# Two graph layers on one core: in layer 0, the next tile's target scores are computed between the maximum and the shift of the softmax

## What is computed

```python
h = einsum('bnd,ade->bane', feat_in, W)
th = tanh(h)
attn = einsum('bane,aeo->bano', th, w_src) + swapaxes(einsum('bane,aeo->bano', th, w_dst), 2, 3)
attn = where(attn >= 0, attn, 0.2 * attn)
attn = softmax(where(~adj, -999.0, attn), axis=-1)
feat_out = elu(einsum('banm,bame->bane', attn, h) + b)
gate = sigmoid(feat_in @ H_w.T + H_b)
return gate * feat_out + (1 - gate) * feat_in
```

## Time and profile before

| what | value |
|---|---|
| runs | 2766.51, 2765.05, 2766.31 us; median 2766.31 |
| the profiled execution's own time | 2766.33 us |
| its span (first to last instruction) | 2764.6 us |
| TensorE matmul busy | 2726.9 us, 99% of the span |
| VectorE busy | 1668.8 us, 60% |
| ScalarE busy | 1160.3 us, 42% |
| GpSimd busy | 1066.3 us, 39% |
| granted TensorE clock | 0.997 of full speed |

### The profile page before, as it was taken

How to read it: one execution, slowest core, us unless ns; L and a number is a source line. 1 busy time by engine, 2 the same in 40 slices (tenths; PEclk the granted TensorE clock), 3 DMA queues, 4 the chain that set the end, 5 groups by cost and what they waited for, 6 DMA issues and landing times.

```text
span 2764.6 us, 51821 instructions
## 1 busy us (share of the span) xinstructions
PE 2726.9 (99%) x20988; PEld 2517.8 (91%) x20988; DVE 1668.8 (60%) x3334; ACT 1160.3 (42%) x3045; POOL 1066.3 (39%) x630
## 2 busy tenths in 40 slices
PE   8999999999999989999999999999999999999998
PEld 6877778888788889999999999999999999999998
DVE  6888998888888754444454444454445445444443
ACT  5666776666666633322332233322332233223322
POOL 2453344433444134433444343434443343434340
PEclk9999999999999999999999999999999999999999
DMA  5656665555555512222213222222222222222220
GB/s 180 173 131 145 164 160 145 139 139 139 141 137 143 175 59 69 69 71 81 70 58 81 76 75 58 79 72 71 69 68 71 81 70 58 81 81 70 58 70 23
DMA packets 306894, 269.49 MB, mean 97 GB/s; under 512 B 227808, under 2 KB 244192, under 8 KB 306656
## 3 DMA queue, kind: packets, MB, share of 16 engines
q1 hardware_dynamic: 306656, 266.19, 35.5%
HBM read 142.65 MB, written 75.89 MB: 79 GB/s over the span
## 4 chain that ended last, share of the span: by engine, by line
PE 85%; DVE 5%; DMA 4%; issue 2%; POOL 2%; ACT 2%; SPq 1%; DVEq 0%; ACTq 0%; POOLq 0%
PE ps_hg L1036 21%; PE ps_a L1199 14%; PE ps_k L70 14%; PE ps_q L70 14%; PE ps_a L70 14%; PE ps_c L1165 2%; PE ps_s L1140 2%; PE ps_pv L1068 1%; DMA dst_all<-dst_scratch 1%; ACT logits L564 1%; PE ps_t L1055 1%; PE ps_pt L1165 1%; DMA dst_scratch<-dst 1%; PE ps_pt L1147 1%; DVE logits L770 1%
## 5 line engine op out<-in xcount | busy, mean ns | idle before, releaser
L1036 PE MATMUL ps_hg<-w_hi,xT 128*128 128x512 f32 x2268 | 745.6, 401 | 8.3 <-DVE h_one L803 8.2
L1036 PEld LDWEIGHTS ps_hg<-w_hi,xT 128*128 128x128 f32 x2268 | 426.1, 188 | 112.6 <-issue 11.3
L1036 PE MATMUL ps_hg<-w_lo,xT 128*128 128x512 f32 x1134 | 448.4, 395 | 0.0
L70 PE MATMUL ps_k<-x1T_hi,wk_hi 128*128 128x256 f32 x1152 | 329.1, 286 | 0.0
L70 PE MATMUL ps_q<-x1T_hi,wq_hi 128*128 128x256 f32 x1152 | 323.5, 281 | 1.4 <-DVE x1T_lo L910 1.4
L70 PE MATMUL ps_q<-x1T_lo,wq_hi 128*128 128x256 f32 x1152 | 322.6, 280 | 0.0
L70 PE MATMUL ps_k<-x1T_lo,wk_hi 128*128 128x256 f32 x1152 | 321.9, 279 | 0.0
L70 PE MATMUL ps_q<-x1T_hi,wq_lo 128*128 128x256 f32 x1152 | 321.9, 279 | 0.0
L70 PE MATMUL ps_k<-x1T_hi,wk_lo 128*128 128x256 f32 x1152 | 321.1, 279 | 0.0
L496 POOL TENSOR_TENSOR th_src<-th,wsrc_all 128x768 f32<-128x768 f32 x64 | 118.3, 1848 | 483.7 <-DVE dst_all L783 463.4
L648 ACT ACTIVATE qT<-ps_q,bq_col 128x256 f32<-128x256 f32 x192 | 80.5, 470 | 479.3 <-PE ps_q L70 479.3
(11 more groups left out here) (144 smaller groups left out, 5814.2 us busy)
## 6 DMA issues: line engine op xcount, KB each, us to landing
x_tok<-x SPq DMA_DIRECT2D x64, 384.0 KB, 4.1
dst_all<-dst_scratch SPq DMA_DIRECT2D x128, 192.0 KB, 3.4
gate_scratch<-gate SPq DMA_DIRECT2D x64, 384.0 KB, 2.6
feat_scratch<-feat SPq DMA_DIRECT2D x128, 192.0 KB, 2.8
feat_in<-feat_scratch SPq DMA_DIRECT2D x62, 384.0 KB, 3.1
gate_in<-gate_scratch SPq DMA_DIRECT2D x62, 384.0 KB, 3.7
x_even<-x SPq DMA_DIRECT2D x16, 768.0 KB, 4.2
x_odd<-x SPq DMA_DIRECT2D x16, 768.0 KB, 4.4
```

Of the source, the lines that this page charges most:

```text
L70: ins = pe.matmul(out, left[a][c], right[b][c], start=(n == 0), stop=(n == len(terms) - 1))
L1036: ins = pe.matmul(ps_hg[:, cols], left[a][c], right[b][c], start=(c == 0 and n == 0), stop=(c == KC - 1 and n == 2))
```

## The change

The shift (line 778) leaves `softmax_scores` and becomes a function of its own, `shift_scores`. In the loop it is called after `dst_scores(T)`, so the target scores of tile T are computed between the maximum and the shift of tile T-1. After the loop, for tile 63, it directly follows `softmax_scores` as before. All waits and signals are the same: the shift waits for `max_done` and raises `shift_done`.

```diff
@@ -774,6 +774,8 @@
                 dve.wait_ge(masked_done, T + 1)
                 dve.tensor_reduce(neg_max[:, :], per_head(logits[:, :], HEADS0), AX_X, ALU.max,
                                   negate=True).then_inc(max_done, 1)
+
+            def shift_scores(T):
                 dve.wait_ge(max_done, T + 1)
                 dve.tensor_tensor(per_head(logits[:, :], HEADS0), per_head(logits[:, :], HEADS0),
                                   over(neg_max[:, :], HEADS0, NODES), ALU.add).then_inc(shift_done, 1)
@@ -881,6 +883,7 @@
                 if T == 1:
                     bias_h(T)
                 dst_scores(T)
+                shift_scores(T - 1)
                 if T >= 2:
                     attention(T - 2)
                     bias_h(T)
@@ -946,6 +949,7 @@
 
             rest_x1(0)
             softmax_scores(NT - 1)
+            shift_scores(NT - 1)
             attention(NT - 2)
             for n in range(3):
                 w1_rest(dve, EARLY_W1 + n)
```

## The result

| | before | after |
|---|---|---|
| median | 2765.68 us (2764.57 to 2766.51) | 2828.06 us (2827.04 to 2830.58) |
| ratio | | 1.0227, 95% interval 1.0209 to 1.0245 |
| span of the profiled execution | 2764.6 us | 2825.5 us |

A forecast was written before the change was run, and what follows sets the result against it. In layer 0 TensorE sets the pace, 14.31 us a tile, until the h_one loop closes at 14.47. +2.8 us to tile 63's multiply and +0.87 at layer 0's end make +3.7 on 2766.33: 2770.0 us, range 2765.0 to 2774.5.

The forecast's parts named there:

- the price of the moved shift: On VectorE behind the target scores' reduction: the shift adds 0.87 us, making multiply to end of h_one 4.81 instead of 3.94.
- the 2.0 us gained at the start: Tiles 1 and 2: multiplies skip the shift ahead of them, so tile 2's comes at 50.48 instead of 52.47.
- the held tiles: Tiles 10 and 12, held by GpSimd's mixing work and late ScalarE: 0.40 and 0.94 us over the loop, written as 1.4.
- The cover that failed: Later work in a tile, GpSimd's product included, was taken as covered by idle time or not delayed, and costed at nothing.
- The loop: Layer 0, each tile: multiply to h_one 4.81, to matmul 0.15, to tanh's end 9.47, to multiply 0.04; 14.47 us against 14.31.
- The 0.87 us at the end of layer 0: Tile 62's shift joins VectorE's chain from tile 63's multiply to the last early weights' split, for which TensorE waits: +0.87 us.
- 0.87 against 0.99: Start-to-start time of VectorE operations: 0.99 us when waiting for the engine's last result, 0.87 otherwise; the forecast took 0.87.
- The exponential: On ScalarE after the shift: ends at 520.12, 0.28 us before the probabilities' weight load at 520.40, so costs nothing.
- The two slower ones (2775.1 and 2777.3): Rivals: VectorE's own length becomes the bound, 2775.1 us, 14%; every VectorE operation costs 0.99 us, 2777.3 us, 2%.
- VectorE's own length: Rival: in tiles with weight splits or mixing work, VectorE's idle time does not absorb the shift; +8.8, 2775.1 us, 14%.
- the forecast's own spread: 2766.8 to 2773.2 us: 1.8 us either way from the loop's terms, 1.4 either way from the held tiles.
- the excess of 0.18 us over what h_one had to spare: In each tile: the shift's 0.87 us exceeds h_one's usable 0.69 us, so the loop closes and 0.16 us is lost.

The follow-up runs named there:

- the two experiments that leave it in its new place: Against the changed kernel: GpSimd's product made to wait for the shift's end, 2782.07 us; or the maximum written to PSUM and read there by the shift, 2773.45 us.
- the PSUM version: The changed kernel with the maximum written to a free PSUM bank, from which the shift reads it: 2773.45 us, ratio 1.0024 to the kernel before.

## Why the prediction was wrong, point by point

- **The step that failed** is the price of the moved shift: "The shift comes behind the reduction, needs the maximum alone, and so costs 0.87 us." That was read from neighbours on VectorE and from what the shift waits for. What ran on another engine at the new place was not asked. The shift costs 1.75 us there, 1.83 less the overlap of some 0.08 with the next instruction, because GpSimd's product, which starts 0.08 us after the multiply's end (515.62 after 515.54), holds it until the product has ended. Put into the forecast's own sum: 61 x (15.35 - 14.47) = 53.7 us for the tiles, 0.88 at the end of layer 0, and 1.5 of the 2.0 us gained at the start were not there (51.99 instead of 50.48). 3.7 + 53.7 + 0.9 + 1.5 = 59.8; the spans differ by 60.9, and 0.9 of the rest is that the held tiles came to 2.3 us instead of 1.4, most of it in the 16.81 us between the multiplies of tiles 2 and 3.
- **The cover that failed** with it: "GpSimd's product waits for the multiply, which is not later." True, and beside the point; the product is not delayed but delays. The trace of before held the warning. On VectorE the ELU's last step reads two tiles in SBUF, the attention's multiply one in PSUM and one in SBUF, and GpSimd is at work beside most of both (before: least, median and most ns):

```profile
L819 DVE SCALAR_TENSOR_TENSOR feat<-att,feat x64: 948/1608/2158, 58.0 to 972.6; 128x768 f32<-128x768 f32 x64
```

```profile
L794 DVE TENSOR_TENSOR att<-ps_pv,row_inv x64: 957/958/960, 54.6 to 963.3; 128x768 f32<-128x768 f32 x64
```

  One varies by a factor of two and the other by 3 ns. The two ELU steps with GpSimd idle beside them take 0.95 and 0.96 us, the other 62 between 0.95 and 2.16. The low part of x (line 752), also with two SBUF inputs, takes 0.94 to 0.96 us in the 18 tiles with GpSimd idle beside it and 1.12 to 1.74 in the other 43. The durations that I used for the new place came from instructions with one SBUF input, or with two and GpSimd idle: beside the shift and the multiply of before GpSimd never works. By the Trainium skill, "SBUF — State Buffer", section "Who interferes with whom", a VectorE instruction with two SBUF inputs contends with a GpSimd instruction that reads SBUF and not with one that only writes; the section calls what they share an exclusive lock and lets the order of issue decide who is blocked. The runs agree on each part: 0.94 us with one input moved to PSUM, 0.96 beside memsets, 0.95 for the shift and 2.50 for the product when the shift starts first. The forecast did not use that rule.
- **The loop was right.** Where the shift keeps its 0.95 us, in the two experiments that leave it in its new place, the tiles take 14.467 and 14.465 us against 14.47 predicted, and the whole is 2773.45 us in the cleaner of them, against 2770.0. Its profiled execution is 6.1 us above the forecast: 1.9 by the multiply of tile 63 (936.41 against 934.55), of which 1.6 at the start, and 4.3 in layer 1, shown above. The 0.87 us at the end of layer 0 held there. In the changed kernel the same loop gives 15.35 with the true price. The 0.15 us from h_one to the matmul and the 9.47 from there to the tanh held.
- **0.87 against 0.99.** The rows were right for this case against the Trainium skill, "VectorE: DVE Perf Modes", section "The DRAIN you can't avoid", where a semaphore costs nothing extra; the same section adds that a next operation that is not held starts earlier, and the forecast left that out. With the shift ahead of the sum, no instruction stands behind its own input there, multiply to end of h_one falls from 4.81 to 4.69, and a tile from 14.465 to 14.347 us.
- **The start**: the multiply of tile 1 did skip the shift (39.23 after 37.49), but the maximum itself stood 0.8 us later than before (37.49 against 36.73) in a part of the program that is the same, behind transfers that landed later, and the multiply of tile 2 came 0.48 us earlier, not 2.0. The other six versions with the shift moved have it at 51.67 to 54.04, the kernel before and the three versions that keep its order at 52.38 to 54.84. These ranges overlap, so what the new order itself gives at the start is not shown.
- **The exponential**: forecast to end 0.28 us before its weight load. With the long shift it ends at 519.14 and TensorE does wait for it, 0.26 us; but this wait takes the place of part of the one for h_one, as forecast, and adds nothing.
- **Rivals.** None held. The two slower ones (2775.1 and 2777.3) had the sign and neither the size nor the mechanism. VectorE's own length did not bind: in the PSUM version the ten tiles with a weight split take 14.46 or 14.47 us but for two (14.65 and 14.53), and in the changed kernel nearly every tile takes 15.34 to 15.38 whether or not it has one, so the loop set the length. No rival had a shift that costs more than 0.99 us.
- **The range.** Its upper end was to be half way to the rival at 2775.1. From 2770.0 that is 2772.6, from the 2773.2 of the forecast's own spread 2774.2; 2774.5 is neither. And the excess of 0.18 us over what h_one had to spare should equal the 0.16 lost per tile; the terms come from different tiles and do not fit closer. Neither matters beside 62 us.

## What to carry to other kernels

Before an instruction is moved, ask what the other engines do at its new place, not only what it waits for: here 1.8 us of GpSimd work, begun just before an instruction with two SBUF inputs, cost some 55 us over 64 tiles (2828.06 against 2773.45 us with one input moved to PSUM). The trace of the old order can tell: compare instructions of that operand kind (both inputs in SBUF) with and without GpSimd beside them, and read a wide spread between least and most as a sign. If the two must meet, start the one on the path first, or put the small input in PSUM.

## What the runs showed of the hardware

- The time for which an instruction is blocked lies inside its recorded duration, and does not show as idle time: shift 1.83 us instead of 0.95, product 2.50 instead of 1.85. The blocked shift ended 0.81 us after the product's end both with a product of 1.84 us and with one of 1.47; the blocked product ended 1.71 us after the shift's end. Both are 0.14 us less than the instruction takes unblocked.
- The hold is per instruction: cut in halves, GpSimd's product let the shift in between, at 1.00 us.
- A broadcast input of 12 numbers per partition counts as a second SBUF input: the shift took 1.83 us with it in SBUF and 0.94 with it in PSUM.
- GpSimd's memsets beside the shift changed neither the shift (0.96 us) nor the time (2765.31 against 2765.65).
